# Attention scores' row maxima: two heads on two row halves of the array, one reduction over two banks

## The reference

```python
n1 = _ln(x, ln1_g, ln1_b)
q = jnp.einsum('btd,mdhk->mbhtk', n1, mha_wq) + mha_bq[:, None, :, None, :]
kk = jnp.einsum('btd,mdhk->mbhtk', n1, mha_wk) + mha_bk[:, None, :, None, :]
v = jnp.einsum('btd,mdhk->mbhtk', n1, mha_wv) + mha_bv[:, None, :, None, :]
scores = jnp.einsum('mbhtk,mbhsk->mbhts', q, kk) / jnp.sqrt(jnp.float32(KD))
attn = jax.nn.softmax(scores, axis=-1)
ctx = jnp.einsum('mbhts,mbhsk->mbthk', attn, v)
mha_out = jnp.einsum('mbthk,mhkd->mbtd', ctx, mha_wo) + mha_bo[:, None, None, :]
```

## Time and profile before

| | |
|---|---|
| median of three runs | 1423.33 us (1421.33 to 1429.55) |
| span of the profiled execution | 1426.9 us |
| PE busy | 1393.6 us, 98% |
| DVE busy | 1092.2 us, 77% |
| ACT busy | 916.4 us, 64% |
| POOL busy | 363.6 us, 25% |
| chain that ended last | PE 69%, issue 8%, DVE 4%, DMA 3%, SP's queue 2% |

### The profile page before, as it was taken

One profiled execution on the slowest core, in us unless ns is written; L12 is line 12 of the kernel. 1 busy time (PEld: TensorE's weight loads), 2 busy tenths in 40 slices (PEclk: granted clock), 3 DMA queues, 4 the chain that ended last, 5 costly groups with the idle time before them and its releaser, 6 DMA issues.

```text
span 1426.9 us, 22218 instructions
## 1 busy us (share of the span) xinstructions
PE 1393.6 (98%) x7666; PEld 716.9 (50%) x7666; DVE 1092.2 (77%) x2299; ACT 916.4 (64%) x1706; POOL 363.6 (25%) x351
## 2 busy tenths in 40 slices
PE   8999899999999999999999999999999999999999
PEld 5643434455454654555445554455545454454456
DVE  5779977987789877987779877797769986786721
ACT  3266557766677666675677765876666766757752
POOL 6512342203313123132241133130331322330000
PEclk9999999999999999999999999999999999999999
DMA  4056037430854127441464308541084413561002
GB/s 116 17 70 95 2 45 107 71 62 16 104 76 76 45 38 112 75 75 31 51 101 69 64 31 101 79 75 46 24 102 70 78 56 45 73 77 46 17 1 89
DMA packets 92308, 90.15 MB, mean 63 GB/s; under 512 B 16483, under 2 KB 87267, under 8 KB 91295
## 3 DMA queue, kind: packets, MB, share of 16 engines
q1 hardware_dynamic: 92196, 88.73, 38.6%
HBM read 35.05 MB, written 4.25 MB: 28 GB/s over the span
## 4 chain that ended last, share of the span: by engine, by line
PE 69%; issue 8%; DVE 4%; DMA 3%; SPq 2%; POOL 1%; ACT 1%; DVEq 0%; POOLq 0%; ACTq 0%
PE psum L881 12%; PE psum L866 12%; PE psum L851 12%; PE psum L819 7%; PE psum L838 6%; PE psum L701 5%; PE psum L452 5%; PE psum L736 3%; DMA qst<-mrow 3%; PE psum L475 2%; SPq L1954 2%; PE psum L563 2%; DVE mx L1378 1%; PE psum L573 1%; DVE x L1293 1%
## 5 line engine op out<-in xcount | busy, mean ns | idle before, releaser
L1378 DVE TENSOR_REDUCE mx<-psum 128x1 f32<-128x512 f32 x1024 | 645.5, 681 | 134.2 <-PE psum L851 133.5
L1677 ACT ACTIVATE prob<-psum 128x512 f32<-128x512 f32 x1024 | 568.2, 600 | 270.8 <-PE psum L881 159.4
L866 PE MATMUL psum<-qst,kst 98*128 98x512 bf16 x1024 | 355.9, 383 | 10.5 <-DMA qst<-mrow 8.7
L851 PE MATMUL psum<-kst,qst 96*128 96x512 bf16 x1024 | 318.8, 381 | 2.9 <-DVE resid L1252 1.3
L881 PE MATMUL psum<-prob,vst 128*17 128x512 f32 x2048 | 248.1, 601 | 2.7 <-ACT prob L1677 2.3
L866 PEld LDWEIGHTS psum<-qst,kst 98*128 98x128 bf16 x1024 | 96.9, 99 | 220.8 <-issue 126.9
L851 PEld LDWEIGHTS psum<-kst,qst 96*128 96x128 bf16 x1024 | 99.0, 98 | 121.2 <-issue 17.9
L881 PEld LDWEIGHTS psum<-prob,vst 128*17 128x17 f32 x2048 | 46.7, 97 | 136.3 <-issue 106.8
L838 PE MATMUL psum<-w,cxT 128*128 128x256 f32 x448 | 105.4, 381 | 0.0
L819 PE MATMUL psum<-n2T,x 128*128 128x512 f32 x224 | 103.0, 592 | 0.0
L1828 POOL CAST parts<-resid 128x512 bf16<-128x512 f32 x64 | 41.0, 640 | 239.9 <-DVE resid L1252 239.9
(11 more groups left out here) (244 smaller groups left out, 1761.5 us busy)
## 6 DMA issues: line engine op xcount, KB each, us to landing
kst<-parts SPq DMA_DIRECT2D x186, 128.0 KB, 4.7
qst<-parts SPq DMA_DIRECT2D x186, 128.0 KB, 5.9
cmat<-G_dram SPq DMA_DIRECT2D x7, 1024.0 KB, 4.6
x<-in_L_ffn_fw SPq DMA_DIRECT2D x14, 512.0 KB, 3.7
w<-in_L_ffn_fw SPq DMA_DIRECT2D x14, 512.0 KB, 4.2
xbuf<-in_x SPq DMA_DIRECT2D x8, 512.0 KB, 5.1
kin<-in_ctx SPq DMA_DIRECT2D x8, 512.0 KB, 4.5
out<-acc SPq DMA_DIRECT2D x7, 512.0 KB, 9.0
```

Of the source, the lines that this page charges most:

```text
L851: e.matmul(psum[:, u.bank, :], qst[0:KROWS, h, t * P:(t + 1) * P], kst[0:KROWS, h, :], start=True, stop=True).then_inc(u.full, 1)
L866: e.matmul(psum[:, u.bank, :], kst[0:KROWS + 2, h, g * P:(g + 1) * P], qst[0:KROWS + 2, h, :], start=True, stop=True).then_inc(u.full, 1)
L1378: e.tensor_reduce(mx[:, qq * QUAD + j, t:t + 1], psum[:, u.bank, :], AX, ALU.max).then_inc(u.free, 1)
L1677: e.activation(prob[:, g % 2, j, :], psum[:, u.bank, :], ACT.Exp).then_inc(u.free, 1)
```

## The change

**Row halves.** The heads of a quad are taken in pairs of an even and an odd one. The stack of an even head has its first four terms on rows 0 to 63, the last two on rows 64 to 95 and the negated maximum on rows 96 and 97, as before. An odd head has the maximum's rows at 0 and 1, zeros to row 31, the last two terms on rows 32 to 63 and the first four on rows 64 to 127. `maximum` multiplies only the four first terms, 64 rows, of both heads of a pair with two matmuls that follow each other, one on rows 0 to 63 and one on rows 64 to 127, into two neighbouring banks. One DVE reduction reads both banks and writes two columns of `mx`. `score` still sums all six terms: 98 rows for even heads, 128 for odd ones. So 1024 matmuls for maxima stay 1024, in 512 pairs, and 1024 reductions of 512 columns become 512 of 2 by 512.

**Banks.** `take` gives each product the bank whose last use is due to end first, by the slot tables; `take_two` does so for two neighbours. Both wait on what held the bank before.

**DMAs.** A piece's stack takes 12 DMAs of 16 rows by 4 heads in place of 6 by 8 heads, in three steps with slots of their own: `s` (terms of the high part), `m` (middle), `r` (the two last terms, on semaphores of their own). `maximum` waits for the first four terms, `score` for the rest. `send_rows` issues four DMAs in place of two. At the start, nine DMAs (`shape_stacks`) write ones and zeros into the stacks in place of three, and POOL's selections are written in twice as many, half as large pieces.

**Slots.** All tables are new. `AHEAD` now counts pairs.

```diff
             def maximum(b, qq, j, t):
-                h, m = qq * QUAD + j, qq * QUAD // H
+                h, m = qq * QUAD + 2 * j, qq * QUAD // H
...
-                u = take("max", b, qq, j, t)
-                e.matmul(psum[:, u.bank, :], qst[0:KROWS, h, t * P:(t + 1) * P], kst[0:KROWS, h, :], start=True,
-                         stop=True).then_inc(u.full, 1)
+                both = banks.take_two(("max", b, qq, j, t), freed_at(clock[0], "max", b))
+                for u in both:
+                    if u.was is not None:
+                        e.wait_ge(u.was.free, u.was.n)
+                u = both[0]
+                for par, bank in enumerate((u.bank, u.bank + 1)):
+                    half = slice(HALF * par, HALF * (par + 1))
+                    ins = e.matmul(psum[:, bank, :], qst[half, at(h + par), t * P:(t + 1) * P], kst[half, at(h + par), :],
+                                   start=True, stop=True)
+                ins.then_inc(u.full, 1)
...
             def score(b, qq, g, j):
                 h, q_ = qq * QUAD + j, b * NQ + qq
                 if g == 0 and j == 0:
-                    e.wait_ge(rows_in[q_ % 2], 32 * (q_ // 2 + 1))
+                    for which in range(2 if b or h >= HC else 0):
+                        e.wait_ge(*rest_loaded(which, h // H, h % H // HC, b))
+                    e.wait_ge(rows_in[q_ % 2], 64 * (q_ // 2 + 1))
                 u = take("score", b, qq, g, j)
-                e.matmul(psum[:, u.bank, :], kst[0:KROWS + 2, h, g * P:(g + 1) * P], qst[0:KROWS + 2, h, :], start=True,
-                         stop=True).then_inc(u.full, 1)
+                e.matmul(psum[:, u.bank, :], kst[0:DEPTH[h % 2], at(h), g * P:(g + 1) * P], qst[0:DEPTH[h % 2], at(h), :],
+                         start=True, stop=True).then_inc(u.full, 1)
...
-                e.tensor_reduce(mx[:, qq * QUAD + j, t:t + 1], psum[:, u.bank, :], AX, ALU.max).then_inc(u.free, 1)
+                e.tensor_reduce(mx[:, qq, :, j, t], psum[:, u.bank:u.bank + 2, :], AX, ALU.max
+                                ).then_inc(u.free, 1)
...
+    def take(self, name, until):
+
         assert name not in self.uses
-        self.uses[name] = Use(self.banks[k], n + 1, self.full[k], self.free[k])
+        k = min(range(self.count), key=lambda k: (self.until(k), self.order[k]))
+        self.counts[k] += 1
+        self.uses[name] = self.hold(k, self.counts[k], until)
         return self.uses[name]
+
+    def take_two(self, name, until):
+
+        assert name not in self.uses
+        k = min(range(self.count - 1), key=lambda k: (max(self.until(k), self.until(k + 1)),
+                                                      max(self.order[k], self.order[k + 1])))
+        self.counts[k] += 1
+        one = self.uses[name] = self.hold(k, self.counts[k], until)
+        return one, self.hold(k + 1, one.n, until, k)
...
+            def stack_term(n, i, landed):
+                m, which, c = PIECES[n]
+                for par in range(2):
+                    o, h0 = first_row(par, i), at(m * H + c * HC + par)
+                    e.dma_start((kst, qst)[which][o:o + KD, h0:h0 + HC // 2, :],
+                                parts[HALF * par:HALF * (par + 1), n % 2, TERMS[which][i], :]).then_inc(landed, 16)
...
                 for r in range(2):
-                    e.dma_start(qst[KROWS + r:KROWS + r + 1, qq * QUAD:(qq + 1) * QUAD, :], mrow[:, q_ % 2, r, :]
-                                ).then_inc(rows_in[q_ % 2], 16)
+                    for par in range(2):
+                        o, h0 = MAXROW[par] + r, at(qq * QUAD + par)
+                        e.dma_start(qst[o:o + 1, h0:h0 + PAIRS, :], mrow[UNITS * par:UNITS * (par + 1), q_ % 2, r, :]
+                                    ).then_inc(rows_in[q_ % 2], 16)
...
-            AHEAD="4111100000341233103011200000010312202101012000110120000020414420"
-                  "0001030121230210102104021021103012203101111110111012100002000000")
+            AHEAD="0202010000012032200020020000101101002010020200000000000000200002"
+                  "0200210001000200020010030120011101100021002000001200000000000000")
```

More of the change, by code:

```diff
@@ L45, with __init__, until, hold @@
 class Use:
-    def __init__(self, bank, n, full, free):
-        self.bank, self.n, self.full, self.free = bank, n, full, free
-class Ring:
-    def __init__(self, banks, full, free):
-        self.banks, self.full, self.free, self.n, self.uses = banks, full, free, 0, {}
-    def take(self, *name):
-        k, n = self.n % len(self.banks), self.n // len(self.banks)
-        self.n += 1
+    def __init__(self, bank, n, full, free, was, until):
+        self.bank, self.n, self.full, self.free, self.was, self.until = bank, n, full, free, was, until
+class Banks:
+    def __init__(self, count, full, free):
+        self.count, self.full, self.free, self.uses = count, full, free, {}
+        self.counts, self.latest, self.order, self.taken = [0] * count, [None] * count, [-1] * count, 0
+    def until(self, k):
+        return self.latest[k].until if self.latest[k] is not None else -1000
+    def hold(self, k, n, until, at=None):
+        at = k if at is None else at
+        self.taken += 1
+        self.order[k] = self.taken
+        self.latest[k] = Use(k, n, self.full[at], self.free[at], self.latest[k], until)
+        return self.latest[k]
+    def take(self, name, until):
         assert name not in self.uses
-        self.uses[name] = Use(self.banks[k], n + 1, self.full[k], self.free[k])
+        k = min(range(self.count), key=lambda k: (self.until(k), self.order[k]))
+        self.counts[k] += 1
+        self.uses[name] = self.hold(k, self.counts[k], until)
         return self.uses[name]
+    def take_two(self, name, until):
[5 more added lines that the diff above has]
+        return one, self.hold(k + 1, one.n, until, k)
 class Steps:
@@ L283, in build @@
         pc = Steps(sem("pool_c"), "acc0 r1")
-        RB, VB = (0, 1, 2, 3, 4, 5, 7), 6
-        bank_full = [sem(f"bank_full_{k}") for k in range(len(RB))]
-        bank_free = [sem(f"bank_free_{k}") for k in range(len(RB))]
-        ring = Ring(RB, bank_full, bank_free)
-        uses = ring.uses
+        VB = 7
+        bank_full = [sem(f"bank_full_{k}") for k in range(VB)]
+        bank_free = [sem(f"bank_free_{k}") for k in range(VB)]
+        banks = Banks(VB, bank_full, bank_free)
+        uses = banks.uses
         SLOTS = NQ * TILES
         weights_in = 16 * (1 + 4 + 3 * M + 2 * M + M + M + 1 + 1 + 1 + 1 + 1)
-        stack_loads = 16 * len(TERMS_K)
+        main_loads, rest_loads = 16 * 2 * MAIN, 16 * 2 * (len(TERMS_K) - MAIN)
+        shape_loads = 16 * (2 * M * H // HC - 1 + 2)
         CARRY, MADE = 9, 118
@@ L373, in build @@
+            SP_S=slots(0, "s4:13 m4:0 r4:2 s5:2 m5:3 r5:0 s6:17 m6:9 r6 s7:0 m7:4 r7"),
+            AHEAD="2010300201100100202020000202020002001000020000201100100001202220"
+                  "0102000000200020102020000200000000010000000030000010100000001100")
         for plan in (FIRST, MIDDLE, LAST):
-            assert len(plan["AHEAD"]) == SLOTS and sum(map(int, plan["AHEAD"])) == SLOTS
+            assert len(plan["AHEAD"]) == SLOTS and sum(map(int, plan["AHEAD"])) == SLOTS // 2
             for engine in ("PE", "ACT", "DVE", "POOL", "SP"):
@@ L433, in parts_read, with rest_read @@
             return loaded(which, m, c, b if n > 1 else b - 1)
+        def rest_read(b, n):
+            m, which, c = PIECES[n - 2]
+            if b == 0 and n < 4:
+                return uses["pick", which, HC - 1].full, uses["pick", which, HC - 1].n
+            return rest_loaded(which, m, c, b if n > 1 else b - 1)
         def over_head(v, n=NG):
@@ L635, in pick @@
                             us[h] = take("pick", which, h)
-                        ins = e.matmul(psum[0:KROWS, us[h].bank, :], chosen[:, which, j, h, :], parts[:, which, j, :],
+                        ins = e.matmul(psum[:, us[h].bank, :], chosen[:, which, j, h, :], parts[:, which, j, :],
                                        start=j == 0, stop=j == 2)
@@ L650, in pick_first @@
                         u = us[which, h]
-                        ins = e.matmul(psum[0:KROWS, u.bank, :], chosen[:, which, j, h, :], parts[:, which, j, :],
+                        ins = e.matmul(psum[:, u.bank, :], chosen[:, which, j, h, :], parts[:, which, j, :],
                                        start=j == 0, stop=j == 2)
@@ L1994, in stage_a @@
                         send_rows(0, 0)
-                    stack(b, n)
+                    yield from stack(b, n)
             def second_half(b):
```

262 lines of the change are left out of this document (168 added, 94 removed), and 12 rows, old and new, of the table DVE_A.

## The result

The changed kernel takes 1439.47 us (median of four runs, 1437.99 to 1442.97) against 1422.36 for the kernel before in the same session (1421.33 to 1429.55). The ratio is 1.0116, with an interval of 1.0092 to 1.0139. Forecast was 1384, range 1360 to 1408; the prediction gave slower a chance of 0.05. The profiled execution has a span of 1438.5 us.

What follows compares the result with a forecast made beforehand. The prediction took PE's own work, busy 98% of the span, as the bound. From 1423.3 us: less 111 for pairs, more 60 for division changes, 8 for bank stalls, 4 for late rows, giving 1384; range 1360 to 1408.

Steps and rivals of the forecast that it cites:

- PE is the bound of the kernel before: Whole kernel: PE, busy 98% of the span, sets the end; a microsecond off PE is one off the time.
- A pair costs what one maximum costs: Maxima on PE: two matmuls on row halves take 0.217 us together; 512 pairs save 111 us.
- Changes of the division: PE's switches between whole array, row halves and column groups: 548 more, 0.22 us in and out, 60 us more.
- Cheaper than I think: Rival: pairs going straight into `values` cost no change and no new stalls come; 1365 us and below, chance 0.12.
- DVE: Reductions over two banks take 1.13 us in place of 1.20: 36 us less on DVE, no direct gain.
- SP and the rows of maxima: SP's queue: twice the DMAs make rows of maxima later, half a microsecond more a period; 4 us, ends 0 and 20.
- the rival of 1452: Rival: rows of maxima come late behind blocks of 12 DMAs, 72 us more; 1452 us, chance 0.04.
- Banks: Dense pairs holding two of seven banks stall PE about 1 us a period; 8 us, ends 0 and 30.
- PE stops at DVE or the banks: Rival: each period loses 3 us more at two or three dense places; 1400 to 1415 us, chance 0.10.
- the ones for the pairs: Signs in PE's trace: maxima start in twos, 0.22 us pair to pair; a score before a pair takes 0.31.
- a period at 161 to 163 us: Sign for the forecast: one period of `MIDDLE` falls to 161 to 163 us, from 167.1.
- waits of PE for `mx` or `mrow` above 30 us: Sign against the forecast: PE's waits for maxima or their rows total above 30 us.

Runs made afterwards that it cites:

- floor_after: The changed kernel, but DVE's reduction and, from the third group of keys on, ACT's exponential read only 64 of 512 columns: 1373.3 us.
- floor_before: The kernel before, but its reduction of a maximum and, from the third group on, its exponential read only 64 of 512 columns: 1404.2 us.
- one_bank_long: The changed kernel, but a pair's matmuls cover 256 keys each, one after the other, into one bank; DVE reads each half twice: 1413.6 us.
- new_tables: The changed kernel, same instructions, but other slots: all three AHEAD strings and some 200 other pieces moved: 1459.5 us.

## Why the prediction was wrong

The forecast was 51 us of PE's own gain less 8 for banks and 4 for rows of maxima, 39 us faster. What came is 31 us of gain less 48 for the readers, 17 us slower.

**PE is the bound of the kernel before**: right. With both readers cut to an eighth it gains 18 us of 1422.

**A pair costs what one maximum costs**: right; two pairs in 0.44 us at 405.01, and without overlap the kernel is 71 us slower.

**Changes of the division**: right in size. 0.20 for in and out against 0.22 taken. A pair that goes straight to `values` does pay a change (0.32 us from its second matmul to the next start, in the median, where 0.22 is usual), so that the rival *Cheaper than I think* was wrong there. Not foreseen was the dearer float32 matmul behind a pair, 97 times 0.10, some 10 us. The pieces make 111 - 548 * 0.09 - 10 = 52 us; the floors show 4.9 a period, 39 in eight, and 31 in the whole. floor_after still has 16.3 us of idle time before maxima (8.4 for L1340, 7.9 for exponentials), floor_before 9.0 us of waits for the rows of maxima; 52 + 9 - 16 = 45 us were due. Of the 14 that are missing some 3 are the clock, and the rest stays open.

**DVE**: right. Two reductions take 2.34 us, 1.12 apart (1.13 forecast), and a period of DVE fell from 135 to 130.

**SP and the rows of maxima**: the term of 4 us was wrong in sign. The wait of 8.7 us is gone, and with it the rival of 1452. A row's issue takes 0.63 us in place of 0.58, and the quads finish early enough.

**Banks**: this step failed. The prediction took 8 us, with 0 and 30 as ends; the readers cost 48 us more than before, 26 of them by the second bank. The rival *PE stops at DVE or the banks* had the mechanism, at 3 us a period beside the 1 us of the forecast; it was 7.8 - 1.1 = 6.7. The working had three faults, which the rows show. It laid only DVE's time against PE's, at the place with most pairs, as if seven banks stood empty there; at 739.93 they are full of scores and transposes, and ACT is the one waited for. It let three waiting pairs cover DVE's lag; already the second pair of a group waits, at 600.72. And it looked at 6 slots in 128, while the idle time has 222 places, some 28 a period. A sum of bank time would have shown the danger, and its parts stood in the rows: a reduction of 0.60 us held one bank, 128 * 0.60 = 77 us of bank time a period; now it is 64 pairs * 2 banks * 1.22 = 156, of 7 * 167 = 1169. The lighter DVE was counted as relief, while its hold on the banks doubled. The sum gives no microseconds, though: in one_bank_long it is 64 * 1.22 = 78 again, as before the change, and the readers still cost 40 us there and 18 in the kernel before. Why these 22 us come with the longer reductions and the new order is not shown.

The Trainium skill, page "TensorEngine Tiling (Array Packing)", has the rule that this step lacked: section "Gotcha 1: PSUM Pressure" says that row tiling raises the pressure on PSUM since row tiles write to different banks, and "PSUM Bottleneck" that tiling speeds up TensorE but not the emptying of PSUM. The runs agree: 26 us for the second bank.

**The signs**: the ones for the pairs came true (starts in twos, 0.31 before a pair). Of the others, PE was to stay above 95% (94%, with records missing), and a period at 161 to 163 us (168.9). The sign *waits of PE for `mx` or `mrow` above 30 us* stood at 17.4 and would have missed the case, because it named DVE and SP and forgot ACT, which holds the same banks.

The clock was in no term of the prediction; it is some 5 of the 17 us.

No version that does all of the work was found to beat the kernel before.

## What to carry to other kernels

When matmuls are put side by side, count bank time (banks held, times the time until their reader is through) for all products that share the pool, before and after: two matmuls in the time of one take twice the banks for each microsecond of PE, and readers that were hidden come out. Test such a change first with its readers cut short, in the old and in the new kernel: the difference is what the matrix engine gains, and the distance to the full kernels is what the banks take back. If shortening either of two readers helps by the same amount and the waits move to the other, suspect the pool between them, and test it by changing the banks alone. The sum of bank time tells which way it goes, not how many microseconds. And compare the granted clocks before explaining the last few microseconds.

## What the runs showed of the hardware beside this

A small copy on DVE took up to eleven times its time beside work of POOL. In new_tables POOL's addition L2007 and DVE's copy L1102 (128 by 16) run at the same time, POOL's row first:

```profile
448.79 2.37 POOL L2007 TENSOR_TENSOR acc<-x,xbuf 128x1024 f32<-128x1024 f32 x1 [26.68 <-DVE x L1357]
```

```profile
449.30 1.88 DVE L1102 COPY gend<-cmat 128x16 f32<-128x16 f32 x1
```

It ended at 451.18, with POOL's instruction (451.16). Six of the seven copies in new_tables start behind the start of that addition; they take 0.75 to 1.88 us, and each ends within 0.04 us of the addition's end. In the changed kernel it took 167 to 170 ns all seven times. POOL was idle in six of them, and in the seventh the copy started first, at 275.64, with the addition 0.13 us behind it:

```profile
L1102 DVE COPY gend<-cmat x7: 167/169/170, 124.9 to 1120.4; 128x16 f32<-128x16 f32 x7
```

In new_tables the seven take 9.7 us in place of 1.2, and ACT waits for the gates behind them (34.0 us in six places). The Trainium skill, page "SBUF — State Buffer", section "🔬 SBUF: two separate sides", says that the port pair shared by GpSimd and some of DVE's operations, those in a two-port mode among them, is an exclusive lock, held for a whole instruction by whichever starts first; these rows agree, with the copy's end 0.02 us behind POOL's. So a table that moves POOL's work has a price on DVE that the slots don't show.
